# A four-layer graph network on one core: PE's work of a group cut in halves and reordered in three passes

## What is computed

```python
def _conv_layer(x, he_attr, row, col, stoich, W, att, bias):   # layer 0, l = 0 and 1
    xt = x @ W
    et = he_attr @ W
    a = xt[row] @ att[:H] + et[col] @ att[H:]
    a = jax.nn.leaky_relu(a, NEG_SLOPE)
    amax = jax.ops.segment_max(a, col, num_segments=E)
    ex = jnp.exp(a - amax[col])
    den = jax.ops.segment_sum(ex, col, num_segments=E)
    alpha = ex / den[col]
...
    m1 = (Binv[col] * stoich * alpha)[:, None] * xt[row]
    eout = jax.ops.segment_sum(m1, col, num_segments=E)
    m2 = (Dinv[row] * stoich * alpha)[:, None] * eout[col]
    nout = jax.ops.segment_sum(m2, row, num_segments=N)
...
# layer 1
    msg_in = jnp.concatenate([x[row], x[col]], axis=-1)
    h = jax.nn.relu(msg_in @ mW1 + mb1)
    messages = h @ mW2 + mb2
    aggregated = jax.ops.segment_sum(messages, col, num_segments=x.shape[0])
```

## Time and profile before

| | us |
|---|---|
| median of 3 runs | 14939.49 (14939.19 to 14949.17) |
| the profiled execution, its own time | 14905.86 |
| its span | 14904.1 |
| busy: PE, PE weight load, DVE, ACT, POOL | 9159.2, 7481.1, 8174.9, 5253.0, 7775.8 |

### The profile page before, as it was taken

The page is one execution under the profiler, slowest core; times in us unless marked ns, Lnnn a source line. Parts: engine busy times, 40 slices in busy tenths (PEclk is TensorE's granted clock), DMA queues, the critical chain, the costliest instruction groups (busy, mean ns, idle before and its releaser), DMA issues. The chain is left out here.

```text
span 14904.1 us, 191958 instructions
## 1 busy us (share of the span) xinstructions
PE 9159.2 (61%) x51661; PEld 7481.1 (50%) x51661; DVE 8174.9 (55%) x30197; ACT 5253.0 (35%) x14885; POOL 7775.8 (52%) x7887
## 2 busy tenths in 40 slices
PE   7885666678865666555543444799955555455554
PEld 5675565566655556544433344677743333333333
DVE  7655555544444555544453222699965555555556
ACT  3443333322223333222211111466644444344343
POOL 2334555466644555466654666488844444344443
PEclk7666666655556666666656666899975555655555
DMA  1111111244432111266653333233323333333332
GB/s 15 12 24 42 37 37 38 48 107 108 109 84 48 38 37 38 59 168 170 167 137 90 111 111 110 72 88 88 88 76 88 91 90 91 88 85 91 89 90 80
DMA packets 612550, 1206.43 MB, mean 81 GB/s; under 512 B 185426, under 2 KB 298544, under 8 KB 610992
## 3 DMA queue, kind: packets, MB, share of 16 engines
q0 software_dynamic: 282368, 575.57, 17.8%
q1 hardware_dynamic: 288768, 523.78, 11.1%
q10 hardware_dynamic: 40368, 94.82, 1.6%
HBM read 958.79 MB, written 234.74 MB: 80 GB/s over the span
## 5 line engine op out<-in xcount | busy, mean ns | idle before, releaser
L585 POOL DMA_INDIRECT WK<-tab,IDX x4640 | 4463.3, 962 | 3600.8 <-issue 1308.1
L1383 POOL DMA_INDIRECT B<-tab,IDX x1856 | 1775.5, 957 | 2028.9 <-ACT B L1513 1232.6
L1402 DVE TENSOR_REDUCE WK<-PS 128x4 f32<-128x1024 f32 x928 | 1131.6, 1220 | 1159.1 <-remote 1035.3
L897 PE MATMUL PS<-WK 128*128 128x129 f32 x5568 | 1135.8, 366 | 772.5 <-ACT WK L1129 666.7
L1528 PE MATMUL PS<-B 27*128 27x512 bf16 x1856 | 772.4, 531 | 1304.7 <-DVE WK L1402 841.2
L860 PE MATMUL PS<-WK,B 128*128 128x2 f32 x3712 | 744.2, 322 | 1303.2 <-DVE WK L773 1292.1
L897 PEld LDWEIGHTS PS<-WK 128*128 128x128 f32 x5568 | 976.7, 264 | 964.6 <-ACT WK L1129 701.8
L860 PEld LDWEIGHTS PS<-WK,B 128*128 128x128 f32 x3712 | 748.5, 299 | 1373.7 <-issue 1372.4
L1513 ACT ACTIVATE B<-B 128x33 f32<-128x33 f32 x5568 | 1211.5, 309 | 7.9
L1561 PE MATMUL PS<-B,H 128*128 128x132 f32 x3712 | 885.0, 431 | 399.6 <-DVE ACC L1415 363.3
L1561 PEld LDWEIGHTS PS<-B,H 128*128 128x128 f32 x3712 | 825.2, 331 | 599.9 <-issue 593.2
(11 more groups left out here) (426 smaller groups left out, 21247.2 us busy)
## 6 DMA issues: line engine op xcount, KB each, us to landing
H<-onehots SPq DMA_DIRECT2D x232, 768.0 KB
B<-onehots SPq DMA_DIRECT2D x232, 384.0 KB
onehots<-B ACTq DMA_DIRECT2D x232, 384.0 KB
WK<-onehots SPq DMA_DIRECT2D x232, 384.0 KB
WK<-tab,IDX POOLq DMA_INDIRECT x4640
onehots<-WK SPq DMA_DIRECT2D x232, 256.0 KB
onehots<-B SPq DMA_DIRECT2D x232, 128.0 KB
B<-tab,IDX POOLq DMA_INDIRECT x1856
```

Of the source, the lines that this page charges most:

```text
L585: po.indirect_dma_start(out=G[:, g % n, k, :], out_offset=None, in_=table, in_offset=bass.IndirectOffsetOnAxis(ap=IDX[:, idx, t:t + 1], ax ...
L897: mm = pe.matmul(AG(r, k // 2), OH[:, r, k, :], R[:, r % 2, k, 0:129], start=k % 2 == 0, stop=k % 2 == 1)
L1383: po.indirect_dma_start(out=eG[:, g % 4, k, :], out_offset=None, in_=tab[TW3], in_offset=bass.IndirectOffsetOnAxis(ap=IDX[:, o, t:t + 1], ...
L1402: ve.tensor_reduce(eM2[:, g, b:b + 2, 2 * i:2 * i + 2, 1] if isinstance(g, int) else eM2[:, bass.ds(g, 1), b:b + 2, 2 * i:2 * i + 2, 1].re ...
```

## The change

Three edits, all in the order or the waits of PE and DVE.

**Pass a.** PE's four scalar products of a group go in two halves, the sum between them; the sum is put one step earlier in the body numbering (lag 6 for 7), as are the two transposes (0 for 1, 1 for 2), and the sweep is 6 long. The ring `aY` has four places in place of two. DVE's four steps on the scores stand behind the product in place of ahead of it.

**Pass f.** The sum and the spread alternate in halves, so the second half of the sum, and its `S.ag`, stand behind the wait for the load.

**Pass c.** PE waits for the adds of the sum before (`S.xb`) ahead of the spread.

```diff
-        aY, aDD, aEX, aEW, aNB = room(fa, 2, 2, 3), room(fa, 8, 6), room(fa, 8, 6), room(fa, 2, 4), room(fa, 1)
+        aY, aDD, aEX, aEW, aNB = room(fa, 4, 2, 3), room(fa, 8, 6), room(fa, 8, 6), room(fa, 2, 4), room(fa, 1)
...
                     ve.tensor_tensor(aR[:, qw, :, 0:128], aG[:, rw, :, 0:128],
                                      aEW[:, qw, :].unsqueeze(2).broadcast_to([128, 4, 128]), ALU.mult).then_inc(S.r, 1)
+                if e:
+                    ge, re_ = e
+                    ve.wait_ge(S.s2, at.s2 + ge + 1)
+                    ve.wait_ge(S.p2, at.p2 + ge)
+                    ve.tensor_tensor(aE, aG[:, re_, :, 128], as2[:, :, 0], ALU.add).then_inc(S.e1, 1)
...
         def a_pe(pe, p):
             at, ring = raised_before(p)
 
+            def node(g, r, ks):
+
+                for k in ks:
+                    mm = pe.matmul(as2[:, k, :], aOT[:, r % 4, 128 * k:128 * k + 128], aY[:, r % 4, k // 2, 1:3],
+                                   start=True, stop=True)
+                return mm
+
             def body(j, u):
...
+                e = turn(j, u, 4)
+                if e:
+                    g, r = e
+                    pe.wait_ge(S.ns, at.ns + g + 1)
+                    pe.wait_ge(S.e3, at.e3 + g)
+                    node(g, r, (0, 1))
+                if f := turn(j, u, 6):
                     g, r = f
                     pe.wait_ge(S.r, at.r + g + 1)
                     pe.wait_ge(S.xb, at.xb + g - 1)
...
                     mm.then_inc(S.ag, 1)
...
+                if e:
+                    node(*e, (2, 3)).then_inc(S.s2, 1)
...
-            sweep(7, body)
+            sweep(6, body)
...
         def f_pe(pe, p):
             at, ring = raised_before(p)
 
+            def sums(g, r, h):
+
+                for k in (2 * h, 2 * h + 1):
+                    mm = pe.matmul(AGb(r, h), fSTo[:, r % 4, k, :], bR[:, r % 2, k, 0:129], start=k % 2 == 0, stop=k % 2 == 1)
+                return mm
+
+            def spread(g, r, h, v):
+
+                for k in (2 * h, 2 * h + 1):
+                    for i in range(3):
+                        mm = pe.matmul(PS[:, 2 + r % 2, k:k + 1], fSTt[:, r % 4, 128 * k:128 * k + 128],
+                                       BP[:, bass.ds(v[h] * 3 + i, 1)], start=i == 0, stop=i == 2)
+                return mm
+
...
+                s, n = turn(j, u, 4), turn(j, u, 1)
+                if s:
+                    g, r = s
+                    pe.wait_ge(S.r, at.r + g + 1)
+                    pe.wait_ge(S.xb, at.xb + g - 1)
+                    sums(g, r, 0)
+                if n:
+                    g, r = n
                     v = blocks(pe, 1, g)
                     streamed(pe, p, g, r)
                     pe.wait_ge(S.p2, at.p2 + g - 1)
...
+                    spread(g, r, 0, v)
+                if s:
+                    sums(*s, 1).then_inc(S.ag, 1)
+                if n:
+                    spread(*n, 1, v).then_inc(S.sv, 1)
...
                     pe.wait_ge(S.z, at.z + g - 1)
+                    pe.wait_ge(S.xb, at.xb + g - 1)
```

More of the change, by code:

```diff
@@ L712, in body @@
                     gm, rm = m
-                    qm = rm % 2
+                    qm, ym = rm % 2, rm % 4
                     vm = blocks(ve, 0, gm)
@@ L718, in body @@
                                      AX.X, ALU.max).then_inc(S.tm, 1)
[L719 to L723, removed]
                 if x:
@@ L782, in body @@
                 if e:
+                    ve.wait_ge(S.e1, at.e1 + ge + 1)
+                    ve.scalar_tensor_tensor(aLR, aE, 0.2, aE, ALU.mult, ALU.max).then_inc(S.e2, 1)
+                if m:
+                    ve.wait_ge(S.m3, at.m3 + gm + 1)
+                    ve.tensor_tensor(aT2, aOLD, aY[:, ym, :, 1:2].broadcast_to([128, 2, 2]), ALU.add).then_inc(S.m4, 1)
+                if e:
+                    ve.wait_ge(S.e2, at.e2 + ge + 1)
+                    ve.tensor_tensor(aE, aLR, as2[:, :, 1], ALU.subtract).then_inc(S.e3, 1)
+                if m:
+                    ve.wait_ge(S.m4, at.m4 + gm + 1)
+                    ve.scalar_tensor_tensor(aY[:, ym, :, 2], aT2[:, :, 1], 0.2, aT2[:, :, 1], ALU.mult,
+                                            ALU.max).then_inc(S.ns, 1)
+                    ve.scalar_tensor_tensor(aY[:, ym, :, 0], aT2[:, :, 0], 0.2, aT2[:, :, 0], ALU.mult,
+                                            ALU.max).then_inc(S.m6, 1)
+                if e:
                     ve.wait_ge(S.e3, at.e3 + ge + 1)
@@ L830, in a_pe @@
             at, ring = raised_before(p)
-            def body(j, u):
[L833 to L840, removed]
+            def node(g, r, ks):
[3 more added lines that the diff above has]
+                return mm
+            def body(j, u):
+                e = turn(j, u, 4)
+                if e:
+                    g, r = e
[3 more added lines that the diff above has]
+                if f := turn(j, u, 6):
                     g, r = f
@@ L847, in body @@
                     mm.then_inc(S.ag, 1)
-                if f := turn(j, u, 2):
+                if e:
+                    node(*e, (2, 3)).then_inc(S.s2, 1)
+                if f := turn(j, u, 0):
+                    g, r = f
+                    pe.wait_ge(S.oh, at.oh + g + 1)
+                    pe.wait_ge(S.ot, at.ot + g)
+                    for k in range(4):
+                        t = pe.transpose(PS[:, 4, 128 * k:128 * k + 128], aOH[:, r, k, :], ident[:, :])
+                    t.then_inc(S.pt, 1)
+                if f := turn(j, u, 1):
                     g, r = f
@@ L854, in body @@
                     t.then_inc(S.xt, 1)
[L855 to L859, removed]
-                        mm = pe.matmul(as2[:, k, :], aOT[:, r % 4, 128 * k:128 * k + 128], aY[:, r % 2, k // 2, 1:3],
-                                       start=True, stop=True)
-                    mm.then_inc(S.s2, 1)
             meet(pe)
-            sweep(7, body)
+            sweep(6, body)
         fb = [[WK[:, 0:8704], 0]]
@@ L1079, in body @@
                     pe.wait_ge(S.p2, at.p2 + g - 1)
-                    for k in range(4):
-                        for i in range(3):
-                            mm = pe.matmul(PS[:, 2 + r % 2, k:k + 1], fSTt[:, r % 4, 128 * k:128 * k + 128],
-                                           BP[:, bass.ds(v[k // 2] * 3 + i, 1)], start=i == 0, stop=i == 2)
-                    mm.then_inc(S.sv, 1)
+                    spread(g, r, 0, v)
[3 more added lines that the diff above has]
+                    spread(*n, 1, v).then_inc(S.sv, 1)
             sweep(4, body)
```

23 lines of the change are left out of this document (3 added, 20 removed).

## The result

The changed kernel takes **14858.52 us** (median of 5 runs, 14828.95 to 14899.09) against 14939.49 for the kernel before (5 runs): ratio 0.9947, 95% interval 0.9927 to 0.9967, 81 us less. The forecast was 14,875. The profiled execution took 14828.95 us, with a span of 14827.2 against 14904.1.

The account below looks back on a forecast made before the run. No engine over 61% busy; PE's late signals during POOL's gather runs bound pass a. Terms -107 (a), 0 (f), +43 (c) sum to -64: 14842 from the profiled 14905.86, 14,875 as median (33.6 higher); range 13,900 to 15,240.

Parts of the forecast that it names:

- The reading of pass a: Pass a: PE's signals, not its work, are late during long gather runs; two groups take 15.17 us, 7.59 each.
- Pass a's term: Both passes a: one cycle in five grows to three groups, 0.23 us less for 464 groups, -107 us.
- (2): Pass a: DVE's wait for the scalar products stands behind the product, worth up to 2.85 us.
- (1): Pass a: PE's signal to DVE stands behind the sum, 1.94 us later after a stall, at most +450 us.
- The count of cycles: Pass a: some cycles already of three groups, one in five after the change; such a cycle takes 20.20 us.
- the bound of +90: Pass f: if the chain from load to load is closed, a group takes 6.8 us in place of 6.41, +90.
- If the four places of the ring give the slack, nothing: Pass f: the load's ring of four absorbs the later signal, so no time is added; the term taken was 0.
- my own sign of the second rival: Pass f: wait for the one-hots' load over 500 us and the pass over 1550 us would show the forecast wrong.
- +43 taken: Pass c: the new wait costs 1.1 us once in each of 77 cycles, +85, or is hidden; half taken.
- The clock: Passes c and f: matmuls held behind waits would run at a slower clock; the sum would hardly change.
- Crowded columns: First rival: PE's crowded columns make pass a's signals late and the change cures it, 14,124 us; chance 0.25.
- Halves that only delay: Second rival: halves only delay signals in f, and perhaps a: 15,073 us, or 15,522 with a's full loss; chance 0.28.

Follow-up runs that it names:

- `landwait`: Kernel before, with POOL in the passes a waiting for the previous group's gathers to land: 14818.0 us, ratio 0.9914.
- `halves`: Kernel before with only the change's PE order in pass a and the `aY` ring of four, DVE's order as before: 14670.5 us, ratio 0.982.
- `a_alone`: Kernel before with only the change's pass a code (PE, DVE and `aY`), on a quick chip: 12138.59 us against 12048.7, ratio 1.0073.
- `after_again`: The whole changed kernel run once more, on a late chip: 14870.43 us against the kernel before's 14948.02, ratio 0.9947.
- `c_alone`: Kernel before with only the change's one wait in pass c, on a quick chip: 12056.36 us against 12048.7, ratio 1.0001.

## Why the prediction came out right, and where not

The time came within 17 us of the forecast. The reading of pass a is borne out, but the closeness is in part luck: each of the three terms was off by 25 to 51 us, and the errors nearly cancel.

- **The reading of pass a: right for this kind of chip, incomplete.** The idle time is lateness of PE's signals while long runs of gathers are in flight; `landwait` and `halves` bear it out. How long a run may be depends on the pause behind it: 0.81 us is not enough after four gathers. What I took for a property of the kernel is one of kernel and chip: on the quick ones the same runs make nothing late. The rule of the Trainium skill that was set against this reading ("SBUF — State Buffer", section "Who interferes with whom": DMA never contends with a compute engine) is not contradicted on the quick chips, where L723 is idle 11.0 us in a pass. On the late ones PE is not slowed either: a sum takes 1.94 us in the kernel before and 2.08 us in `a_alone`. What is late is the signal, of which the rule does not speak.
- **Pass a's term: right size, wrong working.** Forecast -107, measured -147 on the first trace and -112 in `after_again`. But I weighed (2), the product ahead of the wait, as a gain and (1), the signal behind the sum, as a loss of up to 450. Alone, (1) gave 281 us. The step that failed is "where PE starts after a stall the scalar products' signal is later by that": in a loop whose stalls come from POOL running ahead, what holds POOL back pays. And the two parts do not add: the second takes away the pause that the first brings. The count of cycles was wrong too. I read 7.34 us a group, under 7.59, as a sign that some cycles were already of three, but the first pass a has no run of twelve gathers; the mean is lower because of its 40 runs of four, at 7.0 us a group, and because a cycle of two takes 14.9 us on average, not 15.17. In the changed kernel 46 cycles of some 105 are of three, not one in five, and such a cycle takes 21.35 us, not 20.20.
- **Pass f: mis-sized.** 0 taken, +51 measured, some 40 of it from the edit; the bound of +90 had the mechanism. On the quick chip, where nothing else holds the pass, it is +130. "If the four places of the ring give the slack, nothing" was the wrong branch: 492.1 and 511.6 us of DMA wait say there is none. The lags say so too: the sum of group g - 4, which frees the load of g, stands in body g, and the spread that uses it in body g + 1. Pass f came close to my own sign of the second rival, 492.1 us of wait against 500 and 1534 us against 1550.
- **Pass c: +43 taken, +18 measured,** about 10 of it from the edit, and 0 on the quick chip. The 1.1 us for each spread is there; more of it was hidden than half.
- **Sum.** -64 forecast, -77 by the spans, -81 by the medians, because I took a's gain too small by 40, f's loss too small by 51 and c's too large by 25. The error in f and the other two cancel but for 14 us.
- **The clock.** It fell in a, f and c; what that cost on the late chip can't be told. On the quick chip pass a's loss is POOL's longer gathers, +49 and +30 us, and no part of it is shown to be the clock's. I had no term for longer gathers; in the changed kernel too they take 993 ns in place of 955. On the quick chip PE was busy for more of pass a than in the old order (1124 of 1257 us against 913 of 1211) and its clock still fell, from 0.76 to 0.57; why is open. The rule of the Trainium skill, "TensorE: Matmul & The Clock Gate", section "HAM oscillation — how this bites in real kernels", lets the clock fall by gaps; this fall it does not cover.
- **The rivals.** Crowded columns: out on a late chip, by `landwait` (crowded, not late) and the changed kernel (apart, late). Halves that only delay: true in f, the opposite of true in a.

## What to carry to other kernels

When an engine waits "remote" for work that had long been done, look at what another engine issues meanwhile, and try holding that engine back before making the waiting one quicker: on a late chip a memset on POOL between gathers took 6.5% off where every reordering took 2% at most. And before a busy engine at a low clock is called the limit, see who waits for it: in `a_alone` PE was busy for 1124 of 1257 us, and the pass had grown by POOL's gathers. Before such a repair goes in, time the kernel on more than one chip: the pause that gives 3.3% in the passes a on one costs 2.2% on another, and the change of this study, whose a and f parts were both slower on a quick chip, was not run there whole; added up, its parts would make some 230 us more, an estimate, since the parts need not add.

## What the runs showed of the hardware

- The same kernel takes 12,043 to 12,049 us on two chips and 14,924 to 14,948 us in three other sets of runs, and the rows differ above all by remote waits: DVE's L723 idle 11.0 against 479.4 us, a pass e 1213 against 1800, pass d 1398 against 1411. The gathers are not slower: their packets take 149 ns each on average in pass a of the kernel before and of `c_alone`. What does it, and whether it is the chip or the occasion, stays open.
- On the late kind PE's signals lag up to 7.8 us behind the end of its work (an end that the profile models) while POOL issues gathers 0.30 us apart, and in the two stretches read come 1.1 and about 1.6 us after the last of the run. With 1.97 us of pause after every four gathers none was late in the stretch read; with 0.81 us fewer.
- A memset of 128x512 on POOL took 0.54 us and lengthened the step between groups from 0.30 to 0.81 us.
- The fourth gather of a group took 1.19 us on average in the first pass a of `a_alone` and 0.96 in `c_alone`, with no wait ahead of it in either; what lengthens it stays open.
